# Eight unread products of the mask ahead of a wait, in the first six iterations that score

## The reference, cut to what matters

```
q, k, v = layernorm(x), ctx, ctx                # 16 heads of 16 numbers
scores  = (q . k) * 16 ** -0.5                  # masked where k's row > q's row
x = x + softmax(scores) . v
x = x + ffn_with_routed_lora(layernorm(x))      # 8 experts, the best 2
x = x + second_attention(layernorm(x), ctx)     # 8 heads, across the rows' axis
x = x + quantised_mlp(layernorm(x))             # 256 -> 1024 -> 256
```

## Time and profile before

| | |
|---|---|
| median of three runs | 429.84 us |
| the profiled execution's own time | 427.87 us |
| its span, from the first instruction to the last | 425.8 us |
| PE, DVE, ACT, POOL busy | 75%, 74%, 64%, 54% |
| mean granted clock of TensorE | 0.919 |

### The profile page before, as it was taken

How to read it: one execution, slowest core, us unless ns; L and a number is a source line. 1 busy time by engine, 2 the same in 40 slices (tenths; PEclk the granted TensorE clock), 3 DMA queues, 4 the chain that set the end, 5 groups by cost and what they waited for, 6 DMA issues and landing times.

```text
span 425.8 us, 10073 instructions
## 1 busy us (share of the span) xinstructions
PE 317.6 (75%) x3010; PEld 196.9 (46%) x3010; DVE 313.3 (74%) x854; ACT 272.9 (64%) x517; POOL 229.1 (54%) x449
## 2 busy tenths in 40 slices
PE   0133496687699798899999999898777567676673
PEld 0012254354465474655665666555344234344442
DVE  6131453668989789998988989897785467998763
ACT  2122254364576797777877877677455257999995
POOL 6265366765747657476766766234424112676543
PEclk9995886996879999999999999999696698899999
DMA  3646765976537738567676677514332300010111
GB/s 99 190 104 177 243 184 130 270 206 172 155 86 225 205 90 224 137 209 207 155 212 193 167 213 188 149 40 115 76 90 58 89 13 2 0 39 25 39 37 63
DMA packets 73134, 56.16 MB, mean 132 GB/s; under 512 B 5376, under 2 KB 62592, under 8 KB 73088
## 3 DMA queue, kind: packets, MB, share of 16 engines
q1 hardware_dynamic: 68896, 50.87, 43.6%
q10 hardware_dynamic: 4192, 4.73, 3.7%
HBM read 36.45 MB, written 18.87 MB: 130 GB/s over the span
## 4 chain that ended last, share of the span: by engine, by line
PE 31%; DVE 21%; DMA 15%; issue 13%; SPq 9%; ACT 7%; POOL 3%; ACTq 0%; POOLq 0%; DVEq 0%
DMA q<-max_t 8%; DVE max L1604 7%; PE ps_st L1085 4%; PE ps_s L1070 4%; PE ps_u L1115 4%; PE ps_st L1052 3%; SPq L614 3%; PE ps_st L1056 3%; DMA q_parts<-q_t 3%; PE ps_ff L1185 2%; PE ps_u L1099 2%; ACT hid L1554 2%; SPq L615 2%; DMA k_parts<-k_split 2%; PE ps_t L1213 2%
## 5 line engine op out<-in xcount | busy, mean ns | idle before, releaser
L1604 DVE TENSOR_REDUCE max<-ps_s 128x2 f32<-128x512 f32 (+1 forms) x192 | 126.2, 682 | 59.3 <-PE ps_s L1038 34.8
L1353 ACT ACTIVATE p<-ps_st 128x512 f32<-128x512 f32 x128 | 72.3, 596 | 23.0 <-PE ps_st L1085 21.6
L1070 PE MATMUL ps_s<-k,q 96*128 96x256 bf16 x256 | 52.0, 288 | 15.4 <-issue 8.5
L1343 ACT ACTIVATE p<-ps_st 128x512 f32<-128x512 f32 x64 | 38.3, 598 | 34.9 <-PE ps_st L1056 33.9
L1085 PE MATMUL ps_st<-q,k 98*128 98x256 bf16 x256 | 49.3, 291 | 7.1 <-ACT p L1353 3.6
L896 POOL TENSOR_SCALAR var<-mv 128x1 f32<-128x1 f32 x32 | 7.2, 226 | 66.6 <-DVE mv L1693 46.0
L1052 PE MATMUL ps_st<-mask_k,ident_bf 128*128 128x512 bf16 x64 | 27.6, 432 | 18.5 <-DMA q<-max_t 18.5
L1115 PE MATMUL ps_u<-p,v 128*32 128x256 f32 x512 | 37.1, 408 | 1.7 <-issue 1.7
L1357 ACT ACTIVATE xh<-xs,shift,rstd 128x256 f32<-128x256 f32 (+1 forms) x32 | 19.1, 596 | 29.9 <-POOL shift L912 23.1
L1070 PEld LDWEIGHTS ps_s<-k,q 96*128 96x128 bf16 x256 | 20.5, 101 | 34.9 <-issue 21.7
L1034 PE MATMUL ps_s<-mask_q,ident_bf 128*128 128x512 bf16 x64 | 25.8, 403 | 9.4 <-DMA k<-k_parts 9.4
(11 more groups left out here) (149 smaller groups left out, 812.0 us busy)
## 6 DMA issues: line engine op xcount, KB each, us to landing
k_parts<-k_split SPq DMA_DIRECT2D x16, 512.0 KB, 3.7
q<-q_parts SPq DMA_DIRECT2D x32, 256.0 KB, 3.9
k<-k_parts SPq DMA_DIRECT2D x32, 256.0 KB, 3.6
kv_in<-in_kv SPq DMA_DIRECT2D x16, 256.0 KB, 3.5
q_parts<-q_t SPq DMA_DIRECT2D x16, 256.0 KB, 3.5
q<-q_parts SPq DMA_DIRECT2D x32, 128.0 KB, 3.9
k<-k_parts SPq DMA_DIRECT2D x32, 128.0 KB, 3.5
q_parts<-q_split SPq DMA_DIRECT2D x16, 256.0 KB, 2.6
```

What stands on the lines that cost most here:

```text
L1070: last = pe.matmul(out_[:, f * D:(f + 1) * D], q1[0:STK, odd, h * D + f * P:h * D + (f + 1) * P], k1[0:STK, odd, h * D:(h + 1) * D], start ...
L1343: act.activation(p0[:, g, :], ps_st[bank_of(ST_BANKS, f"s0t{g}")][:, :], ACT.Exp, scale=SCALE).then_inc(exp0_done[g], 1)
L1353: act.activation(p1[:, h, :], ps_st[bank_of(ST_BANKS, f"s1t{h}")][:, :], ACT.Exp, scale=SCALE).then_inc(exp1_done[h], 1)
L1604: dve.tensor_reduce(out_, src, AX.X, ALU.max, negate=True).then_inc(done, 1)
```

## The change

In iterations 2 to 7 TensorE makes eight extra products ahead of its wait for `k0` and `q0`. Each is the mask's own product, 128x128 by 128x512 in bf16, into the bank of `ps_s` that group 2 is about to fill. Nothing reads them: the group's own first product starts the bank anew. For that, the bank is taken ahead of the wait for the stacks and not behind it. There are 48 extra products. From iteration 8 on only the place of `take` is different.

```diff
+WARM_ITERATIONS, WARM_PRODUCTS = range(S0[FIRST_S0], 8), 8
...
                 b, odd = at(t, S0[g]), (odd + S0[g]) % 2
                 if b is None:
                     return
+                take(pe, S_BANKS, 2, f"s0_{g}", t)
+                out_ = ps_s[bank_of(S_BANKS, f"s0_{g}")]
                 if g == FIRST_S0:
+                    if isinstance(t, int) and t in WARM_ITERATIONS:
+
+                        for _ in range(WARM_PRODUCTS):
+                            pe.matmul(out_[:, :], ident_bf[:, :], mask_q[:, :, :].rearrange("p g k -> p (g k)"), start=True,
+                                      stop=True, skip_group_check=True)
                     pe.wait_ge(k0_landed, b * 32 + 32)
                     pe.wait_ge(q0_landed, b * 32 + 32)
-                take(pe, S_BANKS, 2, f"s0_{g}", t)
-                out_ = ps_s[bank_of(S_BANKS, f"s0_{g}")]
                 pe.matmul(out_[:, :], ident_bf[:, :], mask_q[:, :, :].rearrange("p g k -> p (g k)"), start=True,
                           stop=False, skip_group_check=True)
```

## The result

The changed kernel takes 434.42 us (median of 20 runs, 428.42 to 439.73) against 427.97 us (median of 20 runs) for the kernel before. The ratio is 1.0132, 95% interval 1.0102 to 1.0162: 5.6 us slower, between 4.4 and 6.9. The ratio leaves out executions over 1.5% above the fastest of their kernel, so it is not quite that of the two medians (1.0151). The forecast was 7.9 us more. The sign is right, and the size is about 2 us too large. The profiled execution of the changed kernel took 436.92 us, 2.5 us above its median, so its span is not to be read as the result.

What follows compares the result with a forecast made beforehand. The bound was taken as an early loop between iterations, period about 15 us, through TensorE and the maxima's transfer. Terms 7.04 + 0.93 = 7.97 us, on 429.84, gave 437.7 us; range 432.0 to 442.5.

Steps and rivals of the forecast that it cites:

- Iteration 2, cost 0: Eight products, 3.44 us, fit inside TensorE's 9.36 us wait for the stack of k: cost 0, gain 0.
- Iterations 3 to 6, 7.04 us: TensorE arrives without idle time; products between `scores0_t` and `scores0` add 1.76 us per iteration, uncovered: 7.04 us.
- the hidden transfer: Rival, chance 0.18: the maxima's transfer hides all 1.76 us in iterations 3, 4 and 5; 2.7 us left, 432.5 us.
- the prediction's own signs: Prediction wrong if starts of iterations 4 to 7 move much less than one set each, or restart at clock 1.00.
- Iteration 7, 0.93 us: Products cost 1.76 us, less the 0.83 us the second attention's maxima transpose waited for DVE: 0.93 us, bounds 0 and 1.76.
- The shift survives: The early shift of 8 us lasts to the end, as busy DVE and TensorE leave later stages little room.
- The clock kept up: Rival, chance 0.07: higher clock carried across waits, slow starts of iterations 4 to 8 save 11.6 us; 426.1 us.
- The page: Profile reading: clock below 1.00 in slices between about 32 and 122 us, near 1.00 for the next 200 us.
- The sum: Iterations 3 to 6 and iteration 7 together: 7.04 + 0.93 = 7.97 us added, forecast 437.7 us.
- the base: Median time of the kernel before, 429.84 us, to which 7.9 us were added.

Runs made afterwards that it cites:

- traces where gaps were filled: Kernel before plus unread products filling TensorE's idle time ahead of the maxima's rows, in two fillings of iterations 3 to 6: 1.0102 and 1.0061.
- third kernel in the gaps: Kernel before plus 26, 22, 6, 3 products ahead of the maxima's rows (iterations 3 to 6) and 12, 10 ahead of `turn_gated` (5, 6): 1.0061.

## Why the prediction was right, and where it was off

**Iteration 2, cost 0.** The products lie in the wait, from 16.42 to 20.0. The group behind them starts as early as before. Right in the trace; in time only bounded (-0.2 to 3.2 us).

**Iterations 3 to 6, 7.04 us.** That TensorE arrives without a wait and that nothing covers the products held: DVE's idle time grew by 1.3 and 2.0 us, about their length. TensorE's work grew by 8.1 us, 1 us more than I had, which the slow clock explains in part: in iteration 4 the eight took 2.15 us, since the first of them still ran at 1.2 GHz, and the four sets together took 7.65 us. The term is mis-sized all the same, because I gave the hidden transfer and the full cost as alternatives. Both act. The hops shrank by 2.7 us over three iterations, which is half of what that rival's 5.3 us would be, and most of it (1.9 us) in the hop before iteration 4. That start was to move by 1.8 us and did not move, which by the prediction's own signs speaks against it; the later starts moved by nearly one set more each. The net is 5.1 us in the traces and 3.5 us (2.2 to 4.7) in time, in place of 7.04.

**Iteration 7, 0.93 us.** 0.9 us measured, -0.9 to 2.8. In accord, not proved; the closeness is luck at this width.

**The shift survives.** The two traces of the change don't agree on this: in one the transposes stay 7 to 10 us late up to the last, in the other they are back within 1.2 us of the kernel before from iteration 11 on. Over all runs 5.6 us are left at the end, about what the early stretch adds. I take this as right for the mean; no trace shows it.

**The clock kept up (the faster rival).** It failed for the reason given: granted clock 0.50 in the wait before iteration 4 and 0.50 to 0.59 behind each restart. But the rule of the Trainium skill, "TensorE: Matmul & The Clock Gate", section "Why this matters for your kernels" (no long idle gap, or the lower clock), agrees with the traces where gaps were filled: with 12 and 6 products around `turn_gated` iteration 5 ran at 1.00 from its start. What my rival had wrong was its price. I turned 11.6 us of slow work into a gain of the kernel; in fact 3.2 and 4.3 us less work of TensorE came to nothing, since the hops grew by 5.3 and 6.0 us.

**The page.** I read the clock as near 1.00 for the 200 us behind 122 us. In the earlier trace rows it holds for about 170 us, and behind 298 us five more slices stand at 6 or 8. It changes nothing in the sum, since no product was added there, but the early stretch is not the only one with a lower clock.

**The sum.** 7.97 us were forecast and 5.6 measured, with 437.7 us against 434.4. Of these 3.3 us, 1.9 come from the base: the median of three runs was 429.84, that of 20 is 427.97. The parts measured alone (3.5, 1.5 and 0.9 us) make 5.9 us, give or take about 3, in accord with the whole; that they meet it so closely is luck.

What stays open: which of the transfers ahead in the DMA engines sets the landing of the rows before iterations 5 and 6, and why products added only 0.7 us (-2.8 to 4.2) once the weights were moved. Only for the length of the hop before iteration 4 was a cause shown, by moving the weights.

## What to carry to other kernels

Look whether the engine really waits at the place where filler is put. A wait in the code is one in the trace only where its row has idle time; here that was one iteration in six, and in the others the filler stood in front of ready work, on the loop. The loop here passes through a small transfer beside bulk, and it had some slack on both sides: what was added before the transfer was partly swallowed, and what was gained before it was not paid out. Such a loop is worth a look for it elsewhere. Test it over several iterations, since one iteration's start can stand still while the cost comes back in the next.

## What the runs showed of the hardware that I had not expected

- A transfer of 4 KB took 1.7 to 7.7 us from issue to landing in this one loop: before iteration 4, 2.08 us with 1 MB of weights moved elsewhere and 5.18 with them; before iteration 6, 3.81 us, and 7.66 when it was issued about 4 us earlier.
- TensorE still restarted at full clock after 2.25 us of idleness behind 22 products (third kernel in the gaps: 0.39 us at 51.84 for a product of 512 columns), but fell to half clock within the next 0.7 us, though it was busy again. Here the fall came behind the idle time, and struck the work that followed it.
- Two executions of the changed kernel differ by 10 us in their spans (434.8 and 424.5), and by 2.4 us from the transpose of iteration 2 to that of iteration 6, with the clock's slow parts and the hops at other lengths each time.
